# A second PSUM bank for the first query/key projections, the q and k projections taken in turn, and a readiness count per query group

## The reference

```python
qkv = x @ W_attn + b_attn
q, k, v = to_heads(split(qkv, 3))          # 16 heads of 64
att = softmax(where(causal, q @ k.T / 8, -inf))
y = (att @ v) @ W_proj + b_proj
x = layernorm(x + y)
W_real = unfold(G1_R, G2_R); W_imag = unfold(G1_I, G2_I)      # 512 x 512 each
out = concat(x_re @ W_real.T - x_im @ W_imag.T, x_re @ W_imag.T + x_im @ W_real.T)
x = layernorm(x + out + bias)
```

## Time and profile before

| | us |
|---|---|
| median of two runs (1450.34 to 1451.89) | 1451.12 |
| the profiled execution, its own time | 1453.66 |
| its span on the slowest core, first to last instruction | 1452.1 |
| spans of the eight cores | 1438.1 to 1452.1 |
| TensorE busy with matmuls | 1130.4 (78%) |
| ScalarE busy | 710.7 (49%) |
| VectorE busy | 505.5 (35%) |
| GpSimd busy | 115.2 (8%) |

### The profile page before, as it was taken

The page is one execution under the profiler, slowest core; times in us unless marked ns, Lnnn a source line. Parts: engine busy times, 40 slices in busy tenths (PEclk is TensorE's granted clock), DMA queues, the critical chain, the costliest instruction groups (busy, mean ns, idle before and its releaser), DMA issues.

```text
span 1452.1 us, 23380 instructions; the slowest of 8 cores (1438.1 to 1452.1 us)
## 1 busy us (share of the span) xinstructions
PE 1130.4 (78%) x8866; PEld 536.0 (37%) x8866; DVE 505.5 (35%) x1007; ACT 710.7 (49%) x842; POOL 115.2 (8%) x137
## 2 busy tenths in 40 slices
PE   2169678877887887299896987788787887759896
PEld 1045234333333333144334533333343333424332
DVE  1145222233223222156574532322322232126475
ACT  1010048767776878345210006687677668815411
POOL 2010100000000000022222000000000000003222
PEclk9999899989898896699898999989889889669898
DMA  8965400000000006340135300000000000652022
GB/s 212 241 103 107 43 1 16 1 16 16 2 15 23 23 2 124 87 175 1 58 131 174 101 1 1 16 16 1 16 15 2 15 16 15 103 160 102 1 116 116
DMA packets 116531, 86.58 MB, mean 60 GB/s; under 512 B 101440, under 2 KB 101576, under 8 KB 115400
## 3 DMA queue, kind: packets, MB, share of 16 engines
q1 hardware_dynamic: 104024, 34.65, 10.9%
q0 software_dynamic: 10912, 37.76, 8.5%
q10 hardware_dynamic: 1488, 12.69, 2.8%
HBM read 52.59 MB, written 26.22 MB: 54 GB/s over the span
## 4 chain that ended last, share of the span: by engine, by line
PE 44%; ACT 17%; DMA 14%; DVE 12%; issue 11%; DVEq 0%; ACTq 0%; SPq 0%; POOLq 0%; POOL 0%
ACT p L547 15%; PE ps_g L461 13%; PE ps_big L740 9%; PE ps_big L528 8%; PE ps_y L599 7%; DMA w2r_d<-w2big 6%; PE ps_big L400 4%; DMA w2i_d<-w2big 3%; DVE x_tok L756 3%; DVE qp L476 3%; DMA x_feat<-ystage_d 2%; DVE stats_sb L763 2%; DMA g_sb<-g2i 2%; DVE stats_sb L767 1%; PE ps_big L727 1%
## 5 line engine op out<-in xcount | busy, mean ns | idle before, releaser
L547 ACT ACTIVATE p<-ps_big,consts 128x1024 bf16<-128x1024 f32 (+3 forms) x640 | 592.3, 986 | 414.5 <-PE ps_big L528 410.0
L461 PE MATMUL ps_g<-x_feat,W_sb 128*128 128x512 bf16 x1024 | 280.2, 403 | 53.3 <-DVE qp L476 47.2
L528 PE MATMUL ps_big<-qp,kp 64*128 64x512 bf16 (+3 forms) x1280 | 238.1, 391 | 98.5 <-ACT p L547 93.0
L563 DVE TENSOR_TENSOR pd<-p,mask_sb 128x256 bf16<-128x256 bf16 x256 | 74.5, 291 | 368.2 <-ACT p L547 280.3
L599 PE MATMUL ps_y<-v_all,p 128*128 128x65 bf16 x3840 | 195.2, 203 | 6.7 <-ACT p L547 6.6
L599 PEld LDWEIGHTS ps_y<-v_all,p 128*128 128x128 bf16 x3840 | 151.1, 103 | 84.3 <-issue 75.4
L528 PEld LDWEIGHTS ps_big<-qp,kp 64*128 64x128 bf16 x1280 | 66.3, 95 | 281.2 <-issue 271.2
L740 PE MATMUL ps_big<-Wp_sb,x_feat 128*128 128x512 bf16 x512 | 120.8, 391 | 38.3 <-DMA x_feat<-ystage_d 38.3
L461 PEld LDWEIGHTS ps_g<-x_feat,W_sb 128*128 128x128 bf16 x1024 | 88.5, 102 | 138.7 <-issue 80.9
L777 ACT ACTIVATE mv_sb<-mv_sb,consts 128x1 f32<-128x1 f32 x64 | 18.9, 295 | 234.5 <-DVE mv_sb L771 234.5
L476 DVE TENSOR_SCALAR kp<-ps_g,bqk 128x512 bf16<-128x512 f32 x64 | 48.0, 749 | 216.7 <-PE ps_g L461 216.7
(11 more groups left out here) (58 smaller groups left out, 601.6 us busy)
## 6 DMA issues: line engine op xcount, KB each, us to landing
xstage<-x_in POOLq DMA_DIRECT2D x32, 512.0 KB, 5.3
x_tok<-x_in POOLq DMA_DIRECT2D x8, 2048.0 KB, 8.9
out<-x_tok SPq DMA_DIRECT2D x32, 512.0 KB, 2.7
wstage<-w_attn ACTq DMA_DIRECT2D x8, 1536.0 KB, 15.5
ystage_d<-yst SPq DMA_DIRECT2D x16, 512.0 KB, 3.9
Wp_sb<-w_proj POOLq DMA_DIRECT2D x8, 256.0 KB, 8.7
Wbig_sb<-w2r_d POOLq DMA_DIRECT2D x8, 128.0 KB, 2.6
w2r_d<-w2big SPq DMA_DIRECT2D x8, 64.0 KB
```

Source lines behind the costliest of these rows:

```text
L461: return t.matmul(ps_g[:], W_sb[:, cc * 3072 + j0:cc * 3072 + j0 + 128], x_feat[:, cc * T + tg * 512:cc * T + (tg + 1) * 512], start=(cc = ...
L528: return t.matmul(ps_big[:, off:off + ln], kpb[e * 64:(e + 1) * 64, kk * 128:(kk + 1) * 128], qpb[e * 64:(e + 1) * 64, pos:pos + ln], star ...
L547: return a.activation(o, i, AF.Exp, bias=consts[:, 0:1], scale=0.125)
L563: return v.tensor_tensor(po_, pp, mm_, ALU.mult)
```

## The change

Three edits in `make_qk_jobs` and the loop that uses it:

- In each prologue (`alt_bank=True`, head pair 0 alone) the jobs of q go to `ps_g` and those of k to `ps_y0`, each bank with its own free count `G[bname]`.
- For all head pairs the jobs run q tg 0, k tg 0, q tg 1, k tg 1 and so on, in place of all q and then all k.
- The score matmuls of group `g_` wait for `vq_ready[g_]`, the evacuation of k tg 1 for group 0 and of k tg 3 for group 1, in place of the head pair's last evacuation for both.

```diff
-        def make_qk_jobs(hp):
+        def make_qk_jobs(hp, alt_bank=False):
             jobs = []
             par = hp % 2
-            for which in range(2):
...
-                for tg in range(NTG):
+            for tg in range(NTG):
+                for which in range(2):
+                    j0 = which * 1024 + 128 * hp
...
+                    bname = ("ps_y0" if (alt_bank and (2 * tg + which) % 2)
+                             else "ps_g")
+                    bank = ps_y[0] if bname == "ps_y0" else ps_g
...
                             if cc == 0:
-                                w_list.append(G["ps_g"])
+                                w_list.append(G[bname])
...
-                            G["ps_g"] = ("dv", vdv)
-                            return vdv
+                            G[bname] = ("dv", vdv)
+                            return (tg if which == 1 else None, vdv)
...
+        tg_need = [((g + 1) * GS * 128) // 512 - 1 for g in range(NG)]
+
+        def consume(job_ret, vq):
+            if job_ret is None:
+                return
+            tg_fin, vdv = job_ret
+            if tg_fin is None:
+                return
+            for g in range(NG):
+                if tg_need[g] == tg_fin:
+                    vq[g] = vdv
...
-        for j in make_qk_jobs(0):
-            r = j()
-            if r is not None:
-                last = r
-        qk_done[0] = last
+        vq0 = [0] * NG
+        for j in make_qk_jobs(0, alt_bank=True):
+            consume(j(), vq0)
+        qk_done[0] = vq0
...
-                                w_list = [("dv", v_qk_ready), G["ps_s%d" % half]]
+                                w_list = [("dv", vq_ready[g_]),
+                                          G["ps_s%d" % half]]
```

More of the change, by code:

```diff
@@ L446, in build, with mm @@
         G["ps_g"] = ("dv", xf_tile[n_tt - 1])
-        def make_qk_jobs(hp):
+        def make_qk_jobs(hp, alt_bank=False):
             jobs = []
             par = hp % 2
-            for which in range(2):
-                j0 = which * 1024 + 128 * hp
-                dstbuf = qp[par] if which == 0 else kp[par]
-                bcol = which * 8 + hp
-                for tg in range(NTG):
+            ji = [0]
+            for tg in range(NTG):
+                for which in range(2):
+                    j0 = which * 1024 + 128 * hp
+                    dstbuf = qp[par] if which == 0 else kp[par]
+                    bcol = which * 8 + hp
+                    bname = ("ps_y0" if (alt_bank and (2 * tg + which) % 2)
+                             else "ps_g")
+                    bank = ps_y[0] if bname == "ps_y0" else ps_g
                     def half(lo, which=which, j0=j0, dstbuf=dstbuf, bcol=bcol,
-                             tg=tg, par=par):
+                             tg=tg, par=par, bname=bname, bank=bank):
                         vpe = 0
                         for cc in range(lo, lo + CC // 2):
-                            def mm(t, cc=cc, j0=j0, tg=tg, x_feat=x_feat):
+                            def mm(t, cc=cc, j0=j0, tg=tg, x_feat=x_feat,
+                                   bank=bank):
                                 return t.matmul(
-                                    ps_g[:],
+                                    bank[:],
                                     W_sb[:, cc * 3072 + j0:cc * 3072 + j0 + 128],
@@ L474, in half, with evq @@
                         if lo > 0:
-                            def evq(v, dstbuf=dstbuf, tg=tg, bcol=bcol):
+                            def evq(v, dstbuf=dstbuf, tg=tg, bcol=bcol,
+                                    bank=bank):
                                 return v.tensor_scalar(
-                                    dstbuf[:, tg * 512:(tg + 1) * 512], ps_g[:],
+                                    dstbuf[:, tg * 512:(tg + 1) * 512], bank[:],
                                     bqk[:, bcol:bcol + 1], None, ALU.add)
@@ L489, in make_qk_jobs @@
             return jobs
+        tg_need = [((g + 1) * GS * 128) // 512 - 1 for g in range(NG)]
[8 more added lines that the diff above has]
+                    vq[g] = vdv
         qk_done = {}
         ys_val = []
-        last = 0
-        for j in make_qk_jobs(0):
-            r = j()
-            if r is not None:
-                last = r
-        qk_done[0] = last
+        vq0 = [0] * NG
+        for j in make_qk_jobs(0, alt_bank=True):
+            consume(j(), vq0)
+        qk_done[0] = vq0
         for hp in range(NPAIR):
             par = hp % 2
-            v_qk_ready = qk_done[hp]
+            vq_ready = qk_done[hp]
             pend = make_qk_jobs(hp + 1) if hp + 1 < NPAIR else []
+            vq_next = [0] * NG
+            qk_done[hp + 1] = vq_next
             job_i = 0
@@ L651, in emit_pv @@
                     if job_i < len(pend):
-                        r = pend[job_i]()
-                        if r is not None:
-                            qk_done[hp + 1] = r
+                        consume(pend[job_i](), vq_next)
                         job_i += 1
```

## The result

The changed kernel takes 1430.8 us (median of nine runs) against 1451.9 us (median of eight runs of the kernel before, two of them those shown above). Two of the nine and three of the eight fell into a slower state that executions here have now and then, whatever the kernel; the ratios, and all medians from here on, are of the others, whose medians are 1430.0 and 1450.7 us. The ratio is 0.9858, with a 95% interval of 0.9845 to 0.987: 1.4% faster, within the 2%. The prediction was 1432.0 us, range 1424 to 1440. The profiled execution took 1432.18 us, its slowest core is now core 1 with a span of 1430.6 us, and the other cores lie between 1415.5 and 1427.9.

A forecast was written before the change was run, and what follows sets the result against it. The kernel was taken as a long series of stages bound by TensorE, or ScalarE beside it. Prologue gains of 9.35 + 9.7 = 19.05 us took the median from 1451.12 to 1432.0 us, 8-in-10 range 1424 to 1440.

The forecast's parts named there:

- The sum: Both prologues together: gains of 9.35 and 9.7 us, 19.05 us in all.
- The second prologue: Second sequence's query/key projection before attention: eight jobs stream as 64 matmuls, 23.16 us becomes 13.81, gain 9.35 us.
- The first prologue: First sequence, after the last weight store: six jobs, one at the lower clock, 12.2 us instead of 21.95; gain 9.7 us.
- the bound of three low jobs: First prologue: clock back only after three jobs, as on core 7; 15.9 us, gain on core 2 only 6.0.
- the rival in which all six stay low: First prologue: all six jobs after the restart at the lower clock; total gain 9.9 us, time 1441.3 us; chance 0.08.
- The idle time before the restart: First prologue: TensorE idle about 7 us, in place of 8.71, before restarting at the same 169.46.
- The added wait: First product into `ps_y0` waits for the last k evacuation; cover 2.0 us, costed at nothing, at most 1.0 us per sequence.
- The order of the jobs: Job order and per-group counts inside the attention loop: cost and gain nothing, 2 us allowed either way.
- Does the gain survive: Attentions after the prologues, 403.37 and 402.53 us, keep their length and move forward whole, later stages with them.
- evacuation and matmuls do overlap: Rival denied this: VectorE reading one bank holds up TensorE writing the next in the prologues; 1446.2 us; chance 0.03.
- The clock stayed at a granted 1.00: Rival said otherwise: alternating banks keeps the clock low in both prologues, 4.9 us slower, 1456.0 us; chance 0.02.
- core 4's values: Rival: transposed load after attention lands on late cores in core 4's 11.92 and 7.28 us; another 10.0 us, 1422.0; chance 0.08.

The follow-up runs named there:

- the second experiment: Changed kernel with one bank in the prologues, job order and group counts kept; against the kernel before, ratio 0.9987 (0.9962 to 1.0012), median 1449.3 us.
- the last two runs: Residual's x loads held until transposed loads landed: on the changed kernel 1422.4 us; with weight staging also moved under attention output tiles 1412.1 us.

## Why the prediction was right

- *The sum*: 19.05 us forecast, 19.2 measured in the two prologues of the slowest cores. The medians fell by 20.7 us; the 1.5 us between come from stretches that the sum left out, and that they are small is in part luck, since the landings alone differ by up to 5 us between cores.
- *The second prologue*: 9.35 us forecast from 64 matmuls at 13.81 us; 9.25 measured. The 0.10 us is a gap between the last projection and the first score.
- *The first prologue*: 9.7 forecast, from 12.2 us after the restart; 12.02 measured on core 1, and 11.85 on core 2 itself (from 21.95: a gain of 10.1). One low job was core 2's share and not every core's: in the kernel before, the clock was back after one job on four cores, after two on cores 4 and 5 and after three on cores 1 and 7. In the changed kernel it was back before the second job ended on all eight (that job took 1.89 to 3.13 us, where 1.89 is a job at the full clock and 3.57 one at the lower), so the bound of three low jobs, and the rival in which all six stay low, did not happen. That the missing pauses bring the clock back sooner is not shown: three cores of the kernel before, with its pauses, had it back within the first job, and five of the streaming ones were well into the second (2.29 to 3.13 us).
- *The idle time before the restart* was forecast at about 7 us and is 10.36 on core 1. I took the store's end from one core of one execution, and core 2's idle time of 8.71 us was the shortest of the eight (up to 12.19); over the cores of the changed kernel's profile it runs from 8.57 to 11.79 us. It cost nothing here, since the restart follows the store either way, but the fall of the projection's waits that I named (some 15 us) came out as 53.2 to 41.6 us, 11.6.
- *The added wait*: no product into `ps_y0` waits for `kp`. Its cover was 2.1 us, as worked out (2.0).
- *The order of the jobs*: nothing lost, nothing won in the loop; the second experiment has the whole of edits two and three at a ratio of 0.9987, with an interval that contains 1. Their effect inside the loop is only a change of name: waits for q become waits for k (19.1 us in 14 places, all in the loop, against 6.0 in 6, all in the prologues).
- *Does the gain survive*: both attentions kept their length to 0.6 us. That was the step on which all else rested.
- *The rivals*: evacuation and matmuls do overlap, at full speed. The clock stayed at a granted 1.00 through 64 matmuls that alternate between two banks, job by job. The Trainium skill ("TensorE: Matmul & The Clock Gate", section "A second HAM failure mode: psum-queue depth-cycling") tells of a kernel that cycles through PSUM banks, whose TensorE idles briefly between its groups of matmuls and whose clock goes up and down; this case's trace does not show it, neither without idle moments nor with the 1.01 us ones of the kernel before. Nor did the clock go to 13/16, as the Trainium skill (same page, section "Seeing it yourself") has it once three cores of a die run dense matmuls. Core 1, the value projection with its transposes and the second prologue in one stretch, in the form of the earlier trace rows, at a mean clock of 1.00:

```profile
775.00:854.18 79.18, 79.18 (x415) 41.85 (x415) 40.29 (x49) 0.00 (x0) 5.28 (x10) 1.00 0.24 74
```

  The transposed load did not fall to core 4's values by itself, but it could be made to, as the last two runs show.

## What to carry to other kernels

A wait of a microsecond that repeats costs all of itself where nothing else fills the queue, as the evacuation wait did in the prologues. The edits that touched only the order moved nothing that the time shows. What the projection's waits inside the loop cost, 22.5 - 10.4 + 19.1 = 31.2 us of TensorE's idle time in the changed kernel, no run here tells, since none gave the loop a second bank. Before adding a bank, compare the evacuation with the job beside it: two banks hid one that was shorter, and four hid nothing more in a steady stream; further banks helped only under a one-time wait. And look at what is issued in the same microsecond as a transfer on the critical path: holding back a load that is not needed yet was worth a third to a half as much as the change, after the time that the later load costs.

## What the runs showed that I had not expected

The landing of the transposed load of 512 KB was 11.8 to 15.3 us in the first sequence with a 2 MB load issued 0.02 us behind it on another queue, 6.7 to 11.8 us in the second with the load 0.5 us behind, and 3.7 to 5.8 us in both with the load held back (two runs). Whether the 0.5 us is what makes the second sequence's landings shorter was not tried. I had taken its length, and its spread between cores, as given. Holding the other load back also narrowed the spread of the cores' spans in the two profiles, from 1415.5 to 1430.6 us to 1409.8 to 1421.7 us.
